# Four graph layers on one core: source indices kept in SBUF, fewer and larger transfers, eight buffers for the gathers of layers 2 and 4

## What is computed

```python
edge_index = jnp.stack([src, dst])
x = _layernorm(x + _L0_gnn_ref(x, edge_index, ...))                      # layer 1
x = _layernorm(x + _L1_gnn_ref(x, edge_index, ...))                      # layer 2
x = _layernorm(x + _L2_gnn_ref(x, node_type_8, src, dst, edge_type_16, ...))  # layer 3
x = _layernorm(x + _L3_gnn_ref(x, edge_index, edge_weight, edge_attr_50, ...))  # layer 4
```

```python
# layer 1: attention with four heads, softmax over each target's edges
e = leaky_relu(a_s[src] + a_d[dst]);  alpha = softmax of e over edges of dst
out = segment_sum(h[src] * alpha, dst) + ...
# layer 2: normalised sum
out = segment_sum(dinv[src] * dinv[dst] * h[src], dst)
# layer 3: attention with eight heads and a scale by edge type
attn = (Q[dst] * K[src]).sum(-1) * rel_scale[edge_rel] / sqrt(DH);  softmax over edges of dst
out = segment_sum(attn * V[src], dst) @ Wo + ...
# layer 4: filters from 50 edge attributes
W = (ssp(edge_attr @ w1.T + b1) @ w2.T + b2) * C(edge_weight)
out = segment_sum(h[src] * W, dst) ...
```

## Time and profile before

| | us |
|---|---|
| median of 3 runs | 11,721.99 |
| lowest, highest | 11,718.76, 11,744.60 |
| the profiled execution | 11,726.19 |
| its span in the trace | 11,724.5 |
| PE busy in it | 6639.1 (57%) |
| POOL busy | 6141.6 (52%) |
| DVE busy | 4980.5 (42%) |
| ACT busy | 1831.8 (16%) |

### The profile page before, as it was taken

How to read it: one execution, slowest core, us unless ns; L and a number is a source line. 1 busy time by engine, 2 the same in 40 slices (tenths; PEclk the granted TensorE clock), 3 DMA queues, 4 the chain that set the end, 5 groups by cost and what they waited for, 6 DMA issues and landing times. The chain is left out here.

```text
span 11724.5 us, 100661 instructions
## 1 busy us (share of the span) xinstructions
PE 6639.1 (57%) x31067; PEld 5661.3 (48%) x31067; DVE 4980.5 (42%) x11243; ACT 1831.8 (16%) x3088; POOL 6141.6 (52%) x6479
## 2 busy tenths in 40 slices
PE   4555555555346666666544545455543677776674
PEld 4444444444336666666434444444432455554453
DVE  4444444444542222222355555555554344443444
ACT  0000000000110000000200000000011444444443
POOL 4455555555126666666345555555520666666662
PEclk6666666666655555555566666666655777777776
DMA  4222222222012222122133333333410222222221
GB/s 132 76 76 77 77 77 74 76 77 77 24 39 54 55 54 55 54 54 55 54 123 122 120 123 123 123 123 122 128 46 13 63 60 61 61 61 60 61 60 39
DMA packets 578005, 881.59 MB, mean 75 GB/s; under 512 B 288015, under 2 KB 382274, under 8 KB 564530
## 3 DMA queue, kind: packets, MB, share of 16 engines
q0 software_dynamic: 232704, 536.56, 16.0%
q1 hardware_dynamic: 329082, 327.61, 9.2%
q10 hardware_dynamic: 15696, 11.01, 0.3%
HBM read 842.21 MB, written 32.40 MB: 75 GB/s over the span
## 5 line engine op out<-in xcount | busy, mean ns | idle before, releaser
L623 POOL DMA_INDIRECT PM<-gat_table,TMP x1616 | 1525.4, 944 | 1487.7 <-PE ps L662 932.7
L2097 POOL DMA_INDIRECT TMP<-schnet_table,TMP x1616 | 1558.5, 964 | 1396.8 <-issue 504.0
L1603 POOL DMA_INDIRECT PM<-hgt_kv_table,TMP x1616 | 1527.5, 945 | 1340.9 <-PE ps L1635 682.8
L1157 POOL DMA_INDIRECT TMP<-gcn_table,TMP x1616 | 1527.7, 945 | 1200.1 <-issue 435.5
L1175 PE MATMUL ps<-rows,PM 16*128 16x8 f32 x3232 | 756.1, 359 | 781.3 <-DVE PM L1223 738.8
L1175 PEld LDWEIGHTS ps<-rows,PM 16*128 16x128 f32 x3232 | 717.9, 323 | 880.6 <-DVE PM L1223 767.5
L1635 PE MATMUL ps<-PM 128*128 128x136 f32 x3232 | 637.2, 366 | 734.9 <-DVE PM L1724 664.7
L1635 PEld LDWEIGHTS ps<-PM 128*128 128x128 f32 x3232 | 586.4, 264 | 771.8 <-DVE PM L1710 700.1
L460 DVE TENSOR_TENSOR AC<-AC,ps 128x128 f32 x404 | 115.7, 286 | 1795.3 <-remote 1181.6
L2124 PE MATMUL ps<-PM 128*128 128x128 f32 x3232 | 607.5, 349 | 446.7 <-issue 273.9
L1182 PE MATMUL ps<-TMP 128*128 128x128 f32 x3232 | 838.3, 441 | 26.5 <-DVE TMP L1217 16.4
(11 more groups left out here) (370 smaller groups left out, 9190.1 us busy)
## 6 DMA issues: line engine op xcount, KB each, us to landing
PM<-local_dst_row SPq DMA_DIRECT2D x101, 1024.0 KB
PM<-local_dst_row SPq DMA_DIRECT2D x202, 512.0 KB
PM<-in_attrT SPq DMA_DIRECT2D x404, 100.0 KB
PM<-gat_table,TMP POOLq DMA_INDIRECT x1616
TMP<-gcn_table,TMP POOLq DMA_INDIRECT x1616
PM<-hgt_kv_table,TMP POOLq DMA_INDIRECT x1616
TMP<-schnet_table,TMP POOLq DMA_INDIRECT x1616
TMP<-in_src_et SPq DMA_DIRECT2D x808, 2.0 KB
```

Source lines behind the costliest of these rows:

```text
L623: pool.indirect_dma_start(out=g[:, par, t, 0:ROW0], out_offset=None, in_=tab0_d, in_offset=bass.IndirectOffsetOnAxis(ap=idx[:, par, t:t + ...
L1157: pool.indirect_dma_start(out=g[:, b, k, :], out_offset=None, in_=tab1_d, in_offset=bass.IndirectOffsetOnAxis(ap=idx[:, b, k:k + 1], axis= ...
L1603: pool.indirect_dma_start(out=g[:, par, t, 0:2 * P], out_offset=None, in_=kv_d, in_offset=bass.IndirectOffsetOnAxis(ap=idx[:, par, t:t + 1 ...
L2097: pool.indirect_dma_start(out=g[:, b, k, :], out_offset=None, in_=tab3_d, in_offset=bass.IndirectOffsetOnAxis(ap=idx[:, b, k:k + 1], axis= ...
```

## The change

Six things:

- `src_idx`, 128 x 1616 indices of 32 bits (827 KB), is loaded once in the start block. All gathers read it there; the `idx` tiles, their loads and their semaphores are gone.
- In layer 1 the breaks between tiles are loaded for four rounds at once, with a semaphore of their own, for which DVE waits ahead of the carry chain.
- In layer 2 the edge types are one transfer of 16 x 8 KB a round, double-buffered, in the memory of `xT`; the relation rows are stored once in four rounds. In layer 3 they are loaded once in four rounds.
- In layer 4 the attributes are one transfer of 400 KB a round, double-buffered.
- In layers 2 and 4 `g` has DEEP = 8 groups, and POOL waits for the group eight before.
- Some small tiles move, since `TMP` shrinks from 6470 to 5658 columns.

```diff
+RELQ = -(-NR // 4)
+DEEP = 2 * SLOTS
...
+        src_idx = sb("src_idx", [P, T], U32)
...
                 sp.dma_start(rel, a["L2_gnn_rel_scale"]).then_inc(ld_rel, 16)
+                sp.dma_start(src_idx[:, :], a["src_et"][:, 0:T]).then_inc(ld_idx, 16)
                 sp.dma_start(WA[:, 0:P], a["L0_gnn_W"]).then_inc(ld_late, 16)
...
                 sp.wait_ge(ld_late, 32)
+                sp.wait_ge(ld_idx, 16)
...
                     def load_breaks(i, par):
-                        sp.dma_start(tbrk[:, par, :, :], tbrk_d[:, bass.ds(i * ROUND, ROUND)].partition_broadcast(H0)).then_inc(brk_ready[par], 16)
...
+                        elif i % 4 == 0:
+                            sp.dma_start(tbrk[:, i // 4 % 2, :, :], tbrk_d[:, i * ROUND:(i + 4) * ROUND].partition_broadcast(H0)).then_inc(tile_brk_ready, 16)
...
-                        for b in range(SLOTS):
-                            sp.wait_ge(g_ready[par][b], 16 * KT * (j + 1))
-                        met(sp, i)
-                        load_idx(i + 2, par)
...
                         dve.wait_ge(carry_mm, 4 * i + 1)
+                        if narrow:
+                            dve.wait_ge(tile_brk_ready, 16 * (i // 4 + 1))
...
-        g = A.take(SLOTS, KT, P)
+        g = A.take(DEEP, KT, P)
...
-                for i in range(NR - 1):
-                    for b in range(SLOTS):
-                        sp.wait_ge(gath[b], 16 * KT * (i + 1))
-                        met(sp, i)
-                        load_idx(i + 1, b)
-                        if b % 2:
-                            sp.wait_ge(ty_done, i * SLOTS + b + 1)
-                            met(sp, i)
-                            load_types(i + 1, b // 2)
+                for i in range(NR - 2):
+                    sp.wait_ge(ty_done, (i + 1) * SLOTS)
+                    load_types(i + 2)
 
             @block.gpsimd
             def _(pool):
                 for i in range(NR):
                     for b in range(SLOTS):
-                        pool.wait_ge(idx_ready[b], 16 * (i + 1))
-                        pool.wait_ge(agg, i * SLOTS + b + 1)
-                        met(pool, i)
+                        n = i * SLOTS + b
+                        if n >= DEEP:
+                            pool.wait_ge(agg, n - DEEP + 1 + SLOTS)
                         for k in range(KT):
                             pool.indirect_dma_start(
-                                out=g[:, b, k, :], out_offset=None, in_=tab1_d,
-                                in_offset=bass.IndirectOffsetOnAxis(ap=idx[:, b, k:k + 1], axis=0)).then_inc(gath[b], 16)
+                                out=g[:, n % DEEP, k, :], out_offset=None, in_=tab1_d,
+                                in_offset=bass.IndirectOffsetOnAxis(ap=src_idx[:, (i * SLOTS + b) * KT + k:(i * SLOTS + b) * KT + k + 1], axis=0)).then_inc(gath[n % DEEP], 16)
...
-                            pe.wait_ge(gath[b], 16 * KT * (i + 1))
+                            pe.wait_ge(gath[par * SLOTS + b], 16 * KT * (j + 1))
...
+                for q in range(RELQ):
+                    rounds_ = range(4 * q, min(4 * q + 4, NR))
+                    if q >= 2:
+                        act.wait_ge(rel_stored[q % 2], 16 * (q // 2))
+                    for i in rounds_:
+                        for b in range(SLOTS):
+                            act.wait_ge(rel_mm, i * SLOTS + b + 2)
+                            nc.scalar.copy(relw[:, q % 2, i % 4, b * KT:(b + 1) * KT, :], rel_ps[b % 2]).then_inc(rel_kept, 1)
+                    act.wait_ge(rel_kept, (rounds_[-1] + 1) * SLOTS + 2)
+                    act.dma_start(rel_d[:, rounds_[0] * ROUND * H2:(rounds_[-1] + 1) * ROUND * H2],
+                                  relw[:, q % 2, 0:len(rounds_), :, :].rearrange("p r t h -> p (r t h)")).then_inc(rel_stored[q % 2], 16)
...
-                for i in range(NR - 1):
-                    for b in range(SLOTS):
-                        sp.wait_ge(z_mm, i * SLOTS + b + 1)
-                        met(sp, i)
-                        load_attr(i + 1, b)
-                        sp.wait_ge(gath[b], 16 * KT * (i + 1))
-                        met(sp, i)
-                        load_idx(i + 1, b)
+                def load_attr(i):
+                    sp.dma_start(attr[:, i % 2, :], a["attrT"][:, i * RW:(i + 1) * RW]).then_inc(attr_ready[i % 2], 16)
+
+                for i in range(2):
+                    load_attr(i)
+                for i in range(NR - 2):
+                    sp.wait_ge(z_mm, (i + 1) * SLOTS)
+                    load_attr(i + 2)
...
-                        pool.wait_ge(idx_ready[b], 16 * (i + 1))
-                        pool.wait_ge(msg_done, i * SLOTS + b + 1)
-                        met(pool, i)
+                        n = i * SLOTS + b
+                        if n >= DEEP:
+                            pool.wait_ge(msg_done, n - DEEP + 1 + SLOTS)
```

More of the change, by code:

```diff
@@ L58 @@
 SP_CAP = 20.0
-TW = 6470
+TW = 5658
 class Steps:
@@ L2193, in program @@
                     softplus(0, 0, 0)
[L2194 to L2200 removed]
+                    rounds(dve, round_, narrow)
                 dve.memset(acc1, 0.0).then_inc(acc_step, 1)
```

212 lines of the change are left out of this document (85 added, 127 removed).

## The result

The change takes 11,695.7 us (median of 14 runs, 11,685.1 to 11,699.5), the kernel before beside it 11,733.8 (14 runs, 11,695.6 to 11,752.4). The ratio is 0.9969, with a 95% interval of 0.9960 to 0.9978: a gain of 0.3%, 36 us by the ratio (the medians are 38 apart), small but clear of the noise, where I had forecast none.

A forecast was written before the change was run, and what follows sets the result against it. TensorE's completion signals, held while POOL streams gathers, bound the kernel, not POOL or buffers. Terms -5.2 + 1.5 + 1 + 1 + 4 + 0 = +2.3 gave 11,724 us median; range 11,370 to 11,900, forecast's own 11,650 to 11,800.

The forecast's parts named there:

- Rivals A and B: Layer 2 (first rival, 11,394 us) or layers 2 and 4 (second, 10,944) become POOL-bound; chances 0.21 (whole or half), 0.07.
- Rival C: Layer 4: longer streams hold signals longer, +2.4 us a round, +242, to 11,966 us; chance 0.19, whole or part.
- Step 1: Index loads go: -1.8 us before layer 1's first gather, -3.4 before layer 3's; other index loads 0.
- Step 2: Index list loaded in the start block: at most +2.9 us, taken as +1.5.
- Step 3: Layer 1: one more DVE wait a round in the carry chain, 0 to +3 us, taken as +1.
- Steps 4 and 5: Layer 2's types and stored rows, layer 3's relation rows: 0; layer 4's 400 KB attributes: +1 us at the first load.
- Step 6: Eight buffers: layer 2 at most +15.2 us or -8, taken as +4; layer 4 +8 to -16, taken as 0.
- D: Layer 4's irregular rhythm shifts half a microsecond a round either way, 50 us; chance 0.53 together with the forecast.

The follow-up runs named there:

- e3: Changed kernel with POOL waiting for the group four before in layers 2 and 4, layer 1's tile breaks loaded every round: 11,627.0 us, ratio 0.9898.
- e2: Kernel before with only the source indices kept in SBUF and the index loads and their waits removed: 11,629.3 us, ratio 0.9901.
- e1: Changed kernel plus one always-satisfied POOL wait per group in layers 2 and 4, per round in layers 1 and 3: 11,760.1 us, ratio 1.0019.
- e8: Changed kernel unaltered, run again in a job where signals were on time: 9,286.5 us beside 9,292.1 for the kernel before, ratio 0.9995.
- e12: Same kernel as e3, repeated in a later job where signals were late, beside the kernel before: 11,626.1 us, ratio 0.9900.

## Why the prediction was wrong

**What bounds the kernel** was read rightly, for the kind of runs that the profile showed: POOL waits for consumers that wait for late signals, and not for a buffer more. The rule in bold in the prediction (on time for 5 to 8 us, then held until 3 to 5 us after the last gather) is too simple. It fits the signals ahead of the ends of POOL's stalls in layers 2 and 3 (3.8 to 3.9 us). Others are late and still come in mid-stream: in the lines behind the result, ACT's copy starts at 5016.10, 6.82 us after PE's product ended at 5009.28, with two gathers of the stream still to come. Layer 2's stall stayed, at 3.2 us and 22.9 us a round, with either distance (e3). Rivals A and B, POOL as the bound, are refuted for held signals; so is, for this kernel, the buffer count that the Trainium skill (Perfetto Trace Analysis, Optimization Strategy) names as a possible reason for consistent bubbles: with eight buffers the bubble stayed. Where signals are free, the kernel before is already bound by POOL, again with four buffers. Rival C didn't come about either: layer 4 has 1.8 stalls a round before and after.

**Step 1** had the -3.4 ahead of layer 3 right (e2 has -3.2). It failed at the sentence that put the other index loads at 0. I costed the transfers, which nobody waits for, and not the wait instruction on POOL. It stood in front of the gather together with the wait for the sums, so that after a stall POOL had one instruction more to go through, 0.5 us (0.74 against 0.24 behind DVE's add; e1 brings the 0.73 back). Satisfied waits in a running stream cost nothing: the gathers stay 1.25 us apart, and where signals are free the kernel with them and the one without take the same time (e8). At the end of a stall it is on the path, once in each of 101 rounds: most of the 43 us in layer 2 and of the 64 in layer 4 (38 and 57 in e2). The same term was worth 0.4 to 0.5 us in the usual rounds of layers 1 and 3, but the short rounds went too, 17 in layer 3 that were each 2 to 4 us under the usual, and layer 3 came out at +18. The prediction used layer 3's mean round (26.9) beside its usual stall (7.87) and never asked why the two don't fit: 20.0 + 7.6 is 27.6.

**Step 2**, with the -1.8 of step 1 for layer 1, stood at -0.3; the first gather came 1.0 us later, and between 0.1 and 1.1 later in the held runs with the list and without a pause. Both are small.

**Step 3** failed: +1 predicted, +55 measured against e3 (48 against e12). Taking the grouped load and its wait out again (e3) brought that back; it had made the round behind it 2.5 us longer, 21 times of 24. I had bounded the duration of the wait and put the load, beside the chain, at 0. By what the load acts on the chain's signals stays open.

**Steps 4 and 5** were right at about 0: e2, with the old transfers, and e3, with the new ones, have layers 2 and 3 within 1 us of each other and layer 4 within 5 (10 with e12). PE's first wait for attributes wasn't the 8.33 of the earlier trace rows but 11.5 us, 3 more where I had said 1.

**Step 6** was right in kind. The tails grew by 11.6 and 14.2 us, where at most 15.2 and 8 were allowed, and the rounds gave 2 to 17 back: +11 by e3 and +20 by e12, against the +4 taken. The long second round that it expected in layer 2 (over 30 us) didn't come; it took 23.2.

Put together: +2 predicted, -31 in the profiled execution. The size that was missed is the wait, some -95 by e2 of the -107 in layers 2 and 4; the losses of 52 and 26 hid two thirds of it. The time fell inside the forecast's own range by luck of that sum. The chance of 0.42 that the prediction gave to a gain lay on rivals A, B and D, not on the mechanism that brought it; D's half a microsecond a round has the size, and names no cause. (Its small terms add up to -31 to +26, not -29 to +27; nothing hangs on that.)

## What to carry to other kernels

Cost a wait by where it stands when the engine comes out of a stall, not by whether it is satisfied: a second wait on the same instruction was half a microsecond on the path once a round, more than the transfers it guarded, which nobody waited for. Judge an edit on its own; here one part of six was worth 1%, and two others took two thirds of it back. And when a profile shows signals that arrive late for no recorded reason, find out in a second job whether they always do, before building on it.

## What the runs showed of the hardware that I had not expected

- The same kernel takes 11,740 or 9,292 us, by job (two chips met both kinds), and nearly constant within a job. The difference is in the arrival of TensorE's signals while POOL issues gathers: 0.04 us after the recorded end in e8, up to 11 us in the earlier trace rows. What sets the kind isn't shown by anything here. Nor is it known whether the recording of a profile plays a part: every time on record comes with a recorded span and clock.
- In the held kind POOL's gap of 1.7 to 3 us after the first gather of a round lets more of the round's signals through on time, and turns 27.1 us a round into 24.8 (layer 3), the gap included. Whether a gap without a wait for a landing does so stays open, as do the best place and length. In layer 1 the rounds became uneven, from 24.4 to 30.6.
- On POOL a gather with two waits starts 0.74 us after the signal and with one 0.24.
